# A one-layer language-model tower on one Trainium2 core: batch 0 by head into stacked rows, quarter maxima, six early banks, unread products, and a new order of the first two batches

## What is computed

```python
h = einsum('bsd,bsde->bse', emb[x], rules[kind[x]])        # token rule
n = layernorm(h)
q = einsum('btd,hrd->bhtr', n, Q); k = einsum('bud,hrd->bhur', n, K)
a = softmax(einsum('bhtr,bhur->bhtu', q, k) / 8)            # 8 heads, 512 x 512
h = h + einsum('bhtd,hde->bte', einsum('bhtu,bud->bhtd', a, n), VO)
m = layernorm(h)
c = one_hot(top2(m @ Wg + bg + bias)) * softmax(top2 values)
h = h + sum_e c_e * (relu(m @ W1_e + b1_e) @ W2_e + b2_e)
```

## Time and profile before

| | us |
|---|---|
| timed runs, median (lowest to highest) | 678.07 (675.84 to 680.62) |
| profiled execution, own time | 675.75 |
| its span | 673.9 |
| TensorE busy | 525.9 (78% of the span) |
| VectorE busy | 409.6 (61%) |
| ScalarE busy | 285.6 (42%) |
| GpSimd busy | 238.1 (35%) |

### The profile page before, as it was taken

The page is one execution under the profiler, slowest core; times in us unless marked ns, Lnnn a source line. Parts: engine busy times, 40 slices in busy tenths (PEclk is TensorE's granted clock), DMA queues, the critical chain, the costliest instruction groups (busy, mean ns, idle before and its releaser), DMA issues.

```text
span 673.9 us, 9098 instructions
## 1 busy us (share of the span) xinstructions
PE 525.9 (78%) x2604; PEld 278.8 (41%) x2604; DVE 409.6 (61%) x970; ACT 285.6 (42%) x548; POOL 238.1 (35%) x395
## 2 busy tenths in 40 slices
PE   0174903797787296999999999999999999988580
PEld 0043802255452133444544544544554454437240
DVE  5621685662225284788868959868857767446521
ACT  0101301055562153546555555565555465652350
POOL 5674057633237500220333224124133232236414
PEclk9985965579998598999999999999999999995976
DMA  8732414722751035440440440431332000000000
GB/s 245 257 89 57 118 36 92 181 62 71 174 141 26 19 78 114 94 96 4 92 96 1 95 103 1 95 79 26 71 79 48 2 9 2 9 1 9 0 9 8
DMA packets 21774, 47.03 MB, mean 70 GB/s; under 512 B 6240, under 2 KB 11552, under 8 KB 21664
## 3 DMA queue, kind: packets, MB, share of 16 engines
q1 hardware_dynamic: 15392, 32.23, 20.2%
q0 software_dynamic: 4752, 8.20, 4.7%
q10 hardware_dynamic: 1584, 6.03, 2.7%
HBM read 9.97 MB, written 11.01 MB: 31 GB/s over the span
## 4 chain that ended last, share of the span: by engine, by line
PE 58%; DVE 16%; issue 10%; ACT 3%; DMA 3%; another core or an unknown queue 3%; POOL 2%; SPq 2%; POOLq 0%; DVEq 0%; ACTq 0%
PE bank L1069 15%; PE bank L1057 10%; PE bank L1041 8%; PE bank L942 6%; PE bank L1027 5%; DVE mx L849 4%; PE bank L1008 4%; PE bank L1002 2%; PE bank L1003 2%; DVE r_sb L867 2%; POOL r_sb L503 2%; DMA front<-in_weights 1%; PE bank L933 1%; PE bank L988 1%
## 5 line engine op out<-in xcount | busy, mean ns | idle before, releaser
L849 DVE TENSOR_REDUCE mx<-bank 128x1 f32<-128x512 f32 x256 | 171.1, 688 | 107.3 <-PE bank L1057 79.0
L503 POOL TENSOR_TENSOR r_sb<-r_sb 128x256 f32<-128x256 f32 (+2 forms) x192 | 99.7, 519 | 287.9 <-DVE r_sb L884 188.1
L560 ACT ACTIVATE prob<-bank 128x512 f32<-128x512 f32 x256 | 138.9, 596 | 68.8 <-PE bank L1041 50.5
L1069 PE MATMUL bank<-prob,xa 128*64 128x512 f32 x512 | 141.5, 631 | 3.6 <-issue 3.6
L1057 PE MATMUL bank<-ks,qs 96*128 96x512 f32 x256 | 123.2, 487 | 25.7 <-DVE mx L849 21.4
L1057 PEld LDWEIGHTS bank<-ks,qs 96*128 96x128 f32 x256 | 50.9, 199 | 144.7 <-issue 122.5
L1041 PE MATMUL bank<-qs,ks 97*128 97x512 f32 x256 | 89.1, 430 | 0.7 <-DMA qs<-negm 0.4
L600 ACT ACTIVATE r_sb<-bank,stay 128x512 f32<-128x512 f32 x64 | 43.1, 687 | 68.3 <-PE bank L1003 68.2
L1041 PEld LDWEIGHTS bank<-qs,ks 97*128 97x128 f32 x256 | 44.0, 195 | 19.4 <-issue 13.0
L942 PE MATMUL bank<-r_sb,eT 128*64 128x64 f32 (+1 forms) x544 | 43.2, 239 | 10.2 <-ACT eT L543 6.8
L942 PEld LDWEIGHTS bank<-r_sb,eT 128*64 128x64 f32 x544 | 38.4, 151 | 17.8 <-issue 9.2
(11 more groups left out here) (137 smaller groups left out, 603.3 us busy)
## 6 DMA issues: line engine op xcount, KB each, us to landing
qs<-qk_h SPq DMA_DIRECT2D x64, 128.0 KB
ks<-qk_h SPq DMA_DIRECT2D x56, 128.0 KB
qs<-qk_l SPq DMA_DIRECT2D x32, 128.0 KB
ks<-qk_l SPq DMA_DIRECT2D x28, 128.0 KB
emb_sorted<-front ACTq DMA_DIRECT2D x4, 608.0 KB
y_sorted<-y_out POOLq DMA_DIRECT2D x19, 128.0 KB, 2.5
e_in<-emb_sorted POOLq DMA_DIRECT2D x9, 256.0 KB, 3.0
emb_sorted<-front ACTq DMA_DIRECT2D x3, 640.0 KB
```

What stands on the lines that cost most here:

```text
L503: nc.gpsimd.tensor_tensor(a[:, at:at + width], src[:, 0:width], src[:, width:2 * width], ALU.add).then_inc(S["pool_chain"], 1)
L560: nc.scalar.activation(prob[:, step % NPROB, u % 2, :], bank[u % NST][:], ACT.Exp, scale=SC).then_inc(S["exp_done"], 1)
L849: V.tensor_reduce(mx[:, u // 16, u % 16:u % 16 + 1], bank[3 + n % 2][:], AX.X, ALU.max).then_inc(S["mx_done"], 1)
L1069: last = M(bank[5][64 * hh:64 * hh + 64, :], xa[:, b % XAR, ut, :], prob[:, (16 * b + k) % NPROB, hh, :], start=(ut == 0), stop=(ut == J - 1))
```

## The change

1. Batch 0 has no `proj`. Each head's queries and keys come from products (`head`) with weights repeated three times (`wd_h`, `wd_l`), which leave the stacked rows in PSUM; ACT copies 96 rows straight into `qs` or `ks`, DVE subtracts in the 32 low rows. No DMAs stack batch 0. ACT and DVE make `wd_h` and `wd_l` once, at the start.
2. Batch 0's maxima are turned by quarters (`mq`, two heads each) and sent as `quarter_row`; its raw scores start at step -5 (= (-1,11)), four units a step.
3. Extra jobs before step -1 use six banks in turn (`SPARE`).
4. `keep_busy` issues products that nobody reads: one beside each of the first three rule groups, four after `xT` of batch 0 and four after `head` 3.
5. Span 1: one `count` after the loop in place of three within; the slots of its last two quarters are worked out together and later; `bring(0,1)` moves between the scatters; its 19 groups run two a step in steps 4 to 13 of batch 0; the gathers of batches 4 to 7 are spread over batches 1 to 4.
6. New places: `xT` and `proj` of batch 1 at (0,4) to (0,6), of batch 2 at (1,2) to (1,4), of batch 3 at (1,9) to (1,13); layer norm of batch 2 at (0,14), of batch 3 at (1,4); raw scores of batch 1 from (0,7), of batch 2 from (1,6).

```diff
-        R_AT = [(-1, 14), (-1, 15)] + [(0, g // 3) for g in range(18)]
+        RULE_AT = [4 + g // 2 for g in range(NG[1] + 1)]
+        HEAD_AT = [-6, -6, -5, -4, -3, -2, -1, 0]
+        QROW_AT = [-3, -1, 1, 4]
+        def pair_at(j):
+            if j < 8:
+                return -5 + j // 2
+            return max(j - LEAD, (j - 8) // 2 - 1 if j < 16 else 7 + (j - 16) // 2 if j < 32 else 22 + (j - 32) // 2 if j < 48 else 0)
...
-            return {1: (0, 2), 2: (0, 13)}.get(nb, (nb - 2, XT))
+            return {0: (-2, 4), 1: (0, 4), 2: (1, 2), 3: (1, 9)}.get(nb, (nb - 2, XT))
...
+            return {0: (), 1: ((0, 4), (0, 5), (0, 5), (0, 6)), 2: ((1, 2), (1, 3), (1, 3), (1, 4)),
+                    3: ((1, 10), (1, 11), (1, 12), (1, 13))}.get(nb, [(nb - 2, k) for k in PROJ])
...
+        SPARE = (6, 7, 0, 1, 2, 5)
+        home = {a: SPARE[n % len(SPARE)] if n < len(early) else 6 + n % RING for n, a in enumerate(order)}
...
+            sp.wait_ge(S["ones_ok"], 1)
+            ones_row(0)
+            for q in range(4):
+                quarter_row(q)
+            sp.wait_ge(S["trow_ok"], 2)
+            ones_row(1)
+            for g in range(4):
+                stack(1, g)
...
             place(1, range(2 * J, 2 * J + QC), 2)
+            bring(0, 1)
             values(0)
+            place(1, range(2 * J + QC, NC), 3)
...
-            for b in range(2, B):
-                bring(1, b)
+            bring(1, 2)
+            bring(1, 3)
...
                 if 2 <= b + 2 < B:
+                    if 4 <= b + 3 < B:
+                        bring(1, b + 3)
                     values(b + 2)
...
-                    if (b, k) == (-2, PROJ[3] + 1):
-                        act.wait_ge(S["qk_lo"], 4)
-                        for g in range(4):
-                            for s, src in enumerate((qk_h, qk_h, qk_l)):
-                                act.dma_start(ks[32 * s:32 * s + 32, 0, 2 * g:2 * g + 2, :].bitcast(F32),
-                                              src[32 * g:32 * g + 32, 2:4, :].bitcast(F32)).then_inc(S[f"stack_{g}"], 16)
...
+                        if kind == "head":
+                            act.wait_ge(S["hd_ps"], i + 1)
+                            act.wait_ge(S["zeroed_1"], 16 * 4)
+                            stacked = ks if i % 2 else qs
+                            nc.scalar.copy(stacked[0:96, 0, i // 2, :], ring(a)[0:96, :]).then_inc(S["hd_hi"], 1)
...
+            run(slots(1, (1,), 2))
+            later = slots(1, (2, 3), 3)
+            next(later)
...
-            N_AT = {1: (0, 0), 2: (0, 10), 3: (0, 14)}
+            N_AT = {1: (0, 0), 2: (0, 14), 3: (1, 4)}
...
+                        if kind == "head":
+                            dve.wait_ge(S["hd_hi"], i + 1)
+                            low = ks[64:96, 0, i // 2, :] if i % 2 else qs[32:64, 0, i // 2, :]
+                            V.tensor_tensor(low, ring(a)[64:96, :] if i % 2 else ring(a)[32:64, :],
+                                            low.bitcast(F32), ALU.subtract).then_inc(S["hd_lo"], 1)
...
+            def keep_busy(spare, n):
+                for _ in range(n):
+                    M(spare[:, 0:256], ident, cst[:, 0:256], start=True, stop=True)
...
+                if kind == "head":
+                    pe.wait_ge(S["xs_ready"], 1)
+                    h = i // 2
+                    o = 4 * (2 * (i % 2) + h % 2) + h // 2
+                    M(out_[0:96, :], wd_h[:, o].rearrange("p r n -> p (r n)"), xs[:, 0, :], start=True, stop=False)
+                    last = M(out_[0:96, :], wd_l[:, o].rearrange("p r n -> p (r n)"), xs[:, 0, :], start=False, stop=True)
...
                     for a in aux_at(b, k):
                         aux(a)
-                    score_tile()
+                        if a in (("xT", 0, 0), ("head", 0, 3)):
+                            keep_busy(bank[3], 4)
+                    while todo:
+                        score_tile()
```

369 lines of the change are left out of this document (218 added, 151 removed).

## The result

The changed kernel takes 709.6 us (median of four, 708.5 to 713.1) where the kernel before takes 679.35 (median of four, 675.8 to 683.3; three of these are the runs of the table ahead). The ratio is 1.045, with a 95% interval of 1.038 to 1.053: slower, by 30 us. The profiled execution took 708.56 with a span of 706.8, against 675.75 and 673.9.

The account below looks back on a forecast made before the run. TensorE bounds the even part (busy 233.5 of 240 us), untouched, so PV (2,0) decides: 306 against 294.73. 675.75 plus the 11.3 loss gives 687; half of the timed median's 2.3 added, 688; range 669 to 699.

Parts of the forecast that it names:

- leg 1: Up to batch 0's layer norm: a shorter second slots call, norm starts at 93.7 instead of 96.50, gain 2.8 us.
- leg 3: Batch 0 without rule groups: PV (0,0) at about 129.5, then DVE's 15.4 us less overlap, PV (0,4) at 144.5.
- legs 4, 5: Rule groups, 69.5 us to step 13's end near 213 to 214; then batch 2's norm stall, PV (1,0) at 228.
- leg 6: Batch 1 waits for rows of maxima behind SP's stacks: PV (2,0) at 306 against 294.73, a loss of 11.3 us.
- leg 2: Batch 0's norm to first exponentials, without DMA stacking: first product at 125.4 against 138.66, gain 13.3 us.
- steps -5 to -2 are 4 x 4.1 = 16.4: From batch 0's first maximum, about 109, to the first exponentials' product: DVE sets 4.1 us a step.
- the copies of ACT hide under DVE: In steps -5 to -2: ACT's two copies a step, under 0.7 us each, add no time to DVE's pace.
- leg 5: Batch 2's layer norm: DVE blocks from 214 to about 222.5, yet PV (1,0) at 228 against 243.76, gain 15.8 us.
- they might come back behind batch 2's norm: Rival: the gathers' late replies return there, or a stack is late again; up to 8 us more, 696; no separate chance.
- 0.7 us for each of the last seven: Batch 0's last seven rule groups read their rule's place at run time; TensorE idles, 5 us in all.
- A lower clock in the front: Rival, steps -5 to -2: about 5.7 us a step instead of 4.1, 6.5 later at batch 0, 694; chance 0.12.
- Faster: Rival, batch 1: short wait for max_row(1,1) makes 688 into 674; with max_row(2,0)'s wait gone, 666; chance 0.16.

Follow-up runs that it names:

- e4: The kernel before with the gathers of batches 4 to 7 issued batch by batch instead of in one row of 24; chip B: 641.0 us, ratio 1.000.
- e1: The changed kernel with SyncE's issues reordered, rows of maxima ahead of later stacked tiles; chip B: 667.4 us, ratio 1.040 to the kernel before.
- e7: The changed kernel without the eight unread products behind batch 0's transposes and head 3: 686.5 us, ratio 1.072 to the kernel before.
- e0: The changed kernel itself, run again on chip B: 686.1 us, ratio 1.073 to the kernel before.
- e9: The changed kernel with SyncE reordered, three rule groups a step, raw maxima of batches 1 and 2 one step later; chip C: 680.6 us, ratio 0.994 to before.
- e11: The same kernel as e4 (the kernel before with the gathers split by batch), on chip D: 661.9 us, ratio 0.971 to the kernel before.

## Why the prediction was right and wrong

It said slower, 688 us, with 699 as its upper end; the time was 709.6. By its own legs, on chip A:

| stretch | predicted | A | B |
|---|---|---|---|
| leg 1: norm of batch 0 | 93.7 | 93.45 | 80.9 |
| legs 2, 3: norm to PV (0,0) | 35.8 | 51.9 | 38.9 |
| leg 3: PV (0,0) to (0,4) | 15.0 | 15.0 | 15.1 |
| legs 4, 5: PV (0,4) to (1,0) | 83.5 | 88.4 | 88.7 |
| leg 6: PV (1,0) to (2,0) | 78 | 79.6 | 79.5 |
| PV (2,0) | 306 | 328.2 | 303.1 |

**Where it failed: leg 2.** Of the 22 us that are missing 16 stand between norm and P V of (0,0). Three of them the trace of B shows too. The first product of line 1165 came 32.4 us behind the norm there (31.7 by my working), but from it to P V it took 6.5 us where I had put 4. The other 13 only A has, in the term "steps -5 to -2 are 4 x 4.1 = 16.4": from the first maximum to that product it is 16.9 us on B and 29.8 on A. The sentence that failed is "the copies of ACT hide under DVE". They do on B; on A they start up to 6.5 us after their products (130.58), and VectorE behind them is busy only 3.7 of 12 us. What delays them stays open. The step behind that sentence treated late replies as a matter of one row: I booked their end in batch 0 as a gain (leg 5), named as a rival only that they might come back behind batch 2's norm, and never asked which other indirect DMAs would now stand beside a chain that passes through ScalarE. The trace of the kernel before had a row for its start as well, beside a row of gathers; it could have been read as the same thing:

```profile
54.65 0.75 ACT L543 COPY eT<-bank 64x256 f32<-64x256 f32 x2 [6.82 <-remote]
```

**Leg 1 was right on A,** 93.45 for 93.7. On B nothing of its gain is left (80.9, and 81.1 in e4): the second `slots` call is shorter there too (2.1 us for 4.5), but it starts 2.3 us later, at 78.84 where e4 has 76.58. Into that stretch falls the one `count` that I took at nothing, with +2 as its bound; whether it is the cause no run shows.

**Leg 5's gain was real.** "I expect most of that back": with the gathers split and nothing else, batch 0 takes 82.2 us on D, where the kernel before took 100.1 on A. It was never the new front's, though, and on a chip without late replies there is nothing to get back. This is why the same edit costs 4.5% on A and 7.3% on B: at P V of (2,0) the changed kernel is 33.5 us behind on A and 43.8 on B (against e4); the difference of 10.3 is what only A gives, 18 of split gathers and 3 of a norm that starts earlier than before, less the 10 by which the new front loses more there than the old one (norm to P V: 13.0 more than on B, against 2.6 more for the old front, 47.2 and 44.6 in e4).

**Legs 4 and 5 were 5 us short.** The steps with rule groups took 72.4 instead of 69.5 us, and from PV (0,14) to (1,0) 16.0 instead of 14. The 69.5 is near by luck in part: the four steps with batch 1's tiles took 38.0 us where my terms make 32.9, the last four 21.8 where they make 25.4. Those last steps are 5.5 us each, which is 2.15 and two groups at 1.70, so the price of a group was right and the 0.7 us for each of the last seven did not arise. The stalls are those announced: 4.0 us for `stack(1,0)`, 12.4 us of VectorE in the layer norm (I had said 8.5), of which TensorE waits 9.4. The norm starts 9.5 us behind PV (0,14) instead of 8.5, and PV (1,0) comes 6.5 us behind it instead of 5.5; TensorE's granted clock is 0.68 in that stretch, but that this is the cause isn't shown.

**Leg 6 was right** in mechanism and place: 18.0 us from stack to row of maxima, holes before line 1165 at (1,7) and (1,15). Its size, 79.6 us for 78, is partly luck: to PV (1,7) it took 37.2 instead of 40.1, and from there to PV (2,0) 42.3 instead of 38, since the six steps with batch 3's projection took 24.0 us where I had 19. One part of how it would show was wrong. I said holes of 13 to 17 and of 7 to 9 us released by `negm`; they are 3.96 and 6.13. The first is broken up: TensorE stands at (1,6) for the stacked tile (4.90) and then for `srow` (5.36), which with the 3.96 makes 14.2. Two of the three, and the second hole, go with SyncE's order (e1); the wait for the stacked tile stays. What a second queue would give, no run shows.

**The rivals.** A lower clock in the front costs nothing on B, as far as e7 lowers it. I had taken the full clock for those steps; it was 0.85 in the mean on B (94 to 113.3 us) and 0.66 on A (105 to 138), where TensorE is busy only 15.5 of 33 us. "Faster" named the right hinge, SyncE's order, and priced it well: 14 and 7 to 8 us for the two waits, where e1 took 20.6 out of batch 1. With it mended the kernel is still 4.0% slower on B, so that rival's 674 was out of reach: it would have needed batch 0 as well.

## What to carry to other kernels

When an engine's work is moved to an earlier place, list what is queued behind its results in program order: two rows of maxima and one of sums behind stacks of the next batch cost 15.4 us of idle time and 4.9 of slower products, and an edit of SyncE's order took that away. When a trace shows replies that come late beside one row of indirect DMAs, look for every other such row, gathers and scatters, ask which chains will stand beside them after the change, and measure on more than one chip. Split such a row with other work in between; each wait between held GpSimd for 1.4 to 4.8 us here.

## What the runs showed of the hardware that I had not expected

- The same program takes 641 to 644 us on B, E and F and 679 to 684 on A, C and D, with the granted clock from 360 to 540 us at 1.00 on both kinds (e0 and e4 on B, e9 on C, e11 on D). Most of the difference lies where the traces show late replies: 16 us up to the layer norm, with the late rows in the first 64 us, and 18 us beside the row of 24 gathers. Only the second part is tested, by e11. A gain of 2.9% on one kind is 0.0% on the other.
- The Trainium skill, page "SBUF — State Buffer", section "Who interferes with whom", says that a DMA never contends with a compute engine. GpSimd's row keeps its pace in the late stretches (one DMA in 1.27 us), and yet a copy of ScalarE starts 11.1 us after its data is there (e11 on D, the row at 62.02; its product ended at 50.91). Taking the row of 24 gathers apart gives 19 us back. Whatever is held up there, the semaphore's way or something else, the rule does not cover it. No run here shows which.
- Where a stall lets TensorE's granted clock fall, it costs more than its own length: e1 took 15.7 us of TensorE's idle time out of batch 1, and batch 1 became 20.6 us shorter. The other 4.9 us are busy time of the same 193 recorded products, at a mean granted clock of 0.91 instead of 0.79.
